# Media keys of the gated layer, for two neighbouring examples at a time

## The reference

```
qn = layernorm(x, ln_q_g, ln_q_b)
q = qn @ Wq * 64 ** -0.5                 # 256 -> 16 heads x 64 = 1024
k, v = split(media @ Wkv)                # 128 -> 1024 each, for 64 media tokens
sim = where(media_mask, q @ k^T, min)    # per head: 256 x 64
out = softmax(sim) @ v
x = x + tanh(attn_gate) * (out @ Wo)
h = gelu(layernorm(x) @ W1) @ W2
x = x + tanh(ff_gate) * h
```

## Time and profile before

| | |
|---|---|
| median of 3 runs | 1388.88 us (1388.78 to 1389.87) |
| profiled execution | 1388.42 us |
| its span | 1386.5 us |
| TensorE busy in the span | 1314.9 us, 95% |
| VectorE, ScalarE, GpSimd busy | 764.6, 473.6, 451.3 us |
| mean granted TensorE clock | 0.98 |

### The profile page before, as it was taken

The page is one execution under the profiler, slowest core; times in us unless marked ns, Lnnn a source line. Parts: engine busy times, 40 slices in busy tenths (PEclk is TensorE's granted clock), DMA queues, the critical chain, the costliest instruction groups (busy, mean ns, idle before and its releaser), DMA issues.

```text
span 1386.5 us, 26030 instructions
## 1 busy us (share of the span) xinstructions
PE 1314.9 (95%) x10995; PEld 1055.5 (76%) x10995; DVE 764.6 (55%) x1361; ACT 473.6 (34%) x785; POOL 451.3 (33%) x558
## 2 busy tenths in 40 slices
PE   7977899999999999999999999989899999999988
PEld 5755677787886777888888888876678787787766
DVE  4455575666666656353344434445667566666553
ACT  3323333423324223244345443433332333313321
POOL 1143444444344332211111111324334344334332
PEclk9978999999999999999999999999999999999999
DMA  9010000000001001200000000011000000000000
GB/s 324 7 61 1 2 2 2 1 2 1 2 6 42 2 20 39 86 17 1 1 0 1 0 1 0 1 41 42 2 2 2 1 17 1 2 16 2 1 17 17
DMA packets 19903, 27.31 MB, mean 20 GB/s; under 512 B 3433, under 2 KB 15553, under 8 KB 19521
## 3 DMA queue, kind: packets, MB, share of 16 engines
q1 hardware_dynamic: 19008, 24.20, 5.2%
q10 hardware_dynamic: 768, 1.26, 0.3%
HBM read 23.35 MB, written 2.10 MB: 18 GB/s over the span
## 4 chain that ended last, share of the span: by engine, by line
PE 84%; DVE 6%; ACT 4%; POOL 3%; issue 2%; DMA 0%; SPq 0%; ACTq 0%; DVEq 0%; POOLq 0%
PE bank L1418 6%; PE bank L1708 6%; PE bank L1673 5%; PE bank L1678 5%; PE bank L1562 5%; PE bank L1914 4%; PE bank L1878 4%; PE bank L1921 4%; PE row_banks L1512 4%; PE row_banks L1822 3%; PE row_banks L1545 3%; PE bank L1480 3%; PE bank L1697 3%; PE bank L1411 3%; PE row_banks L1517 2%; ACT room L2032 2%
## 5 line engine op out<-in xcount | busy, mean ns | idle before, releaser
L1269 POOL TENSOR_SCALAR_AFFINE_SELECT room<-room 128x1024 f32<-128x1024 f32 x64 | 70.7, 1108 | 186.4 <-ACT room L2032 186.4
L2274 DVE TENSOR_REDUCE room<-row_banks 128x4 f32<-128x512 f32 (+1 forms) x128 | 116.4, 952 | 23.4 <-PE row_banks L1517 23.0
L2032 ACT ACTIVATE room<-row_banks 128x1536 f32<-128x1536 f32 x64 | 92.9, 1451 | 89.6 <-PE row_banks L1545 89.6
L1708 PE MATMUL bank<-room,down_w 128*128 128x256 f32 x384 | 94.4, 386 | 0.5 <-DVE room L2374 0.5
L2288 DVE RECIPROCAL room<-bank 128x256 f32<-128x256 f32 x32 | 56.1, 1754 | 59.3 <-PE bank L1562 59.3
L2064 ACT ACTIVATE room<-bank 128x256 f32<-128x256 f32 x96 | 36.4, 383 | 147.7 <-PE bank L1678 136.7
L1231 POOL TENSOR_TENSOR room<-room 128x256 f32<-128x256 f32 x32 | 24.5, 766 | 171.8 <-ACT room L2044 171.8
L1708 PEld LDWEIGHTS bank<-room,down_w 128*128 128x128 f32 x384 | 69.6, 190 | 13.6 <-issue 4.9
L1342 POOL TENSOR_TENSOR room<-room 128x512 f32<-128x512 f32 x32 | 33.7, 1070 | 133.1 <-DVE room L2474 132.9
L1545 PE MATMUL row_banks<-room 32*128 32x256 f32 (+1 forms) x1024 | 62.1, 357 | 9.7 <-ACT room L2032 4.6
L1545 PEld LDWEIGHTS row_banks<-room 32*128 32x128 f32 x1024 | 48.9, 191 | 27.6 <-issue 15.6
(11 more groups left out here) (242 smaller groups left out, 3037.8 us busy)
## 6 DMA issues: line engine op xcount, KB each, us to landing
out_x<-wq SPq DMA_DIRECT2D x8, 256.0 KB, 2.3
qkv<-in_L_xattn_v_qkv SPq DMA_DIRECT2D x2, 768.0 KB, 6.4
qkv<-in_L_xattn_l_qkv SPq DMA_DIRECT2D x2, 768.0 KB, 9.2
gate_w<-in_L_xattn_v_gate SPq DMA_DIRECT2D x2, 640.0 KB, 8.4
gate_w<-in_L_xattn_l_gate SPq DMA_DIRECT2D x2, 640.0 KB, 7.6
up_w<-in_L_xattn_v_up SPq DMA_DIRECT2D x2, 640.0 KB, 6.2
up_w<-in_L_xattn_l_up SPq DMA_DIRECT2D x2, 640.0 KB, 6.5
down_w<-in_L_xattn_v_down SPq DMA_DIRECT2D x2, 640.0 KB, 6.4
```

The lines of the kernel that those rows point to most:

```text
L1269: pool.affine_select(out=diagonal, in_=diagonal, compare_op=ALU.is_ge, fill=0.0, base=0, pattern=[[0, 8], [1, P]], channel_multiplier=-1)\
L1708: return pe.matmul(ff_bank[0][:, t * S:(t + 1) * S], down_w[:, f, t * P:(t + 1) * P], hid[:, i, :], start=(i == t == 0), stop=(i == UPS - ...
L2032: act.activation(probs[w % 2], row_banks[:, :, 0:3 * P], ACT.Exp).then_inc(*ATT_ACT.does(e, f"exp{w}"))
L2274: last = dve.tensor_reduce(dst, row_banks[:, :, P * i:P + S * i], X, ALU.max, negate=True)
```

## The change

The keys of examples e and e+1 (e even) are made together. The moving operand is now the 128 media tokens of both, so eight products of 128 columns replace two times eight of 64. As their result has 1024 columns, it is made in two sets of four products that both go to att_bank: the second set waits until VectorE has taken out the first. Each set is taken out in two instructions as before, now with the two examples as one more dimension. k_diag has 2 x 1024 columns, one half per example; v_diag gets a place of its own, which makes the room 1024 columns larger and adds a memset. Waits are changed to match: a_center and n0_sum wait for a_keys_out only after an even example, otherwise for a_scaled; the scores wait for their own half of the keys; the eviction waits for the scores of the example before that read the same half. In the plan the stages a_keys and a_keys_out now have a list of starts of their own, and stand where they stood for the even examples, the second set 0.1 later on TensorE and 0.3 later on VectorE. In the table of stage names, a_keys now counts `k#` and a_keys_out `k#0 k#1`.

```diff
@@ -787,7 +787,6 @@
     put(-824.5585, "a_centered")
     put(-809.0481, "a_mean")
     put(-808.6594, "a_scaled")
-    put(-804.7289, "a_keys_out")
     put(-803.1344, "a_vals_out", 0)
     put(-790.9899, "a_shift", 0)
     put(-790.6773, "a_vals_out", 1)
@@ -819,7 +818,6 @@
     put(1053.9518, "a_center")
     put(1079.5231, "a_sum")
     put(1088.8030, "a_spread")
-    put(1088.9990, "a_keys")
     put(1089.6066, "a_q", 0)
     put(1090.1252, "a_q", 1)
     put(1090.1254, "a_vals", 0)
@@ -838,6 +836,20 @@
     put(1114.2236, "a_turn", 3)
     put(1122.3099, "a_values", 2)
     put(1122.3100, "a_values", 3)
+    return at
+
+
+def keys_stages():
+
+    at = []
+
+    def put(time, stage, *which):
+        at.append((time, stage, *which))
+
+    put(-804.7289, "a_keys_out", 0)
+    put(-804.4289, "a_keys_out", 1)
+    put(1088.9990, "a_keys", 0)
+    put(1089.0990, "a_keys", 1)
     return at
 
 
@@ -940,6 +952,7 @@
 LATE_STARTS = [[3754.298, 3883.620, 4009.349, 4213.053],
                [4720.064, 4857.234, 4982.216, 5129.719]]
 GATED_STARTS = [4135.764, 4249.007, 4285.180, 4322.416, 4357.961, 4394.327, 4430.914, 4466.419]
+KEYS_STARTS = [4135.764, 4285.180, 4357.961, 4430.914]
 GATED_FF_STARTS = [4379.262, 4415.403, 4452.679, 4488.240, 4524.635, 4561.193, 4596.717, 4630.575]
 FINAL_STARTS = [4340.081, 4340.799, 4473.868, 4474.460, 4603.277, 4604.468, 4766.775, 5969.870]
 
@@ -968,6 +981,7 @@
                      for time, stage, *which in late_stages(layer))
     each(FINAL_STARTS, final_stages(), B)
     each(GATED_STARTS, gated_stages())
+    order.extend((KEYS_STARTS[e // 2] + time, stage, e, *which) for e in range(0, B, 2) for time, stage, *which in keys_stages())
     each(GATED_FF_STARTS, gated_ff_stages())
     return [(stage, e, *which) for _time, stage, e, *which in sorted(order)]
 
@@ -1034,7 +1048,7 @@
         media_u8 = sb("media_u8", [P, B * M], U8)
 
 
-        ROOM = 23828
+        ROOM = 24852
         room = sb("room", [P, ROOM])
 
         def two(ap):
@@ -1077,9 +1091,9 @@
         f_mem = ff_room[:, 2304:3328].rearrange("p (a n) -> p a n", a=4)
         turns = take(6 * KT * S)
         q_sb, k_sb, q_cos, q_sin, k_cos, k_sin = (two(turns[:, KT * S * i:KT * S * (i + 1)]) for i in range(6))
-        k_diag = turns[:, 0:1024].rearrange("p (j i m) -> p j i m", j=GT, i=2)
-        v_diag = turns[:, 1024:2048].rearrange("p (j n) -> p j n", j=GT)
-        a_zero = turns[:, 0:2048]
+        k_diag = turns[:, 0:2048].rearrange("p (b j i m) -> p b j i m", b=2, j=GT, i=2)
+        v_diag = take(GT * P).rearrange("p (j n) -> p j n", j=GT)
+        a_zero, v_zero = turns[:, 0:2048], v_diag
         n0_yl, n0_yv, ff_yl, ff_yv, ctx_v, ctx_l = (take(KT, S) for _ in range(6))
         ff_late = take(KT, 2, M)
         a_yl, a_y, b_yl, b_y = n0_yl, n0_yv, ff_yl, ff_yv
@@ -1326,6 +1340,7 @@
                 def a_zero_pads(e):
                     pool.wait_ge(*QKV_ACT.did(B - 1, "qm1"))
                     pool.wait_ge(*QKV_ACT.did(B - 1, "ka1"))
+                    pool.memset(v_zero, 0.0)
                     pool.memset(a_zero, 0.0).then_inc(*A_POOL.does(e, "zero"))
 
                 def a_add(e):
@@ -1440,7 +1455,7 @@
                         pe.wait_ge(*F_ACT.did(0, "m3"))
                         pe.wait_ge(*X_ACT.did(B - 1, "x"))
                     elif e == B:
-                        pe.wait_ge(*A_DVE.did(B - 1, "k1"))
+                        pe.wait_ge(*A_DVE.did(B - 1, "scaled"))
                     elif e % B > 2:
                         pe.wait_ge(*ATT_DVE.did(e - 3, "ctx1"))
                     sum_squares(n0_sq, att_bank).then_inc(*N0_PE.does(e, "sumsq"))
@@ -1796,7 +1811,7 @@
                     if e == 0:
                         pe.wait_ge(*ATT_DVE.did(B - 1, "ctx1"))
                     else:
-                        pe.wait_ge(*A_DVE.did(e - 1, "k1"))
+                        pe.wait_ge(*(A_DVE.did(e - 1, "k11") if e % 2 else A_DVE.did(e - 1, "scaled")))
                     center(e, att_bank).then_inc(*A_PE.does(e, "mu"))
 
                 def a_sum(e):
@@ -1823,14 +1838,18 @@
                                              start=(k == 0), stop=(k == KT - 1))
                     last.then_inc(*A_PE.does(e, f"q{u}"))
 
-                def a_keys(e):
-                    pe.wait_ge(*A_DVE.did(e, "scaled"))
-                    if e == 0:
-                        pe.wait_ge(ca_in, 16 * CA_DMAS)
-                    for j in range(GT):
-                        last = pe.matmul(att_bank[:, j * M:(j + 1) * M], wkv[:, j * P:(j + 1) * P],
-                                         ctx_t[:, e * M:(e + 1) * M], start=True, stop=True)
-                    last.then_inc(*A_PE.does(e, "k"))
+                def a_keys(e, h):
+                    if h == 0:
+                        pe.wait_ge(*A_DVE.did(e, "scaled"))
+                        if e == 0:
+                            pe.wait_ge(ca_in, 16 * CA_DMAS)
+                    else:
+                        pe.wait_ge(*A_DVE.did(e, "k01"))
+                    for j in range(4):
+                        at = (4 * h + j) * P
+                        last = pe.matmul(att_bank[:, j * P:(j + 1) * P], wkv[:, at:at + P],
+                                         ctx_t[:, e * M:(e + 2) * M], start=True, stop=True)
+                    last.then_inc(*A_PE.does(e, f"k{h}"))
 
                 def a_vals(e, c):
                     pe.wait_ge(*A_ACT.did(e, f"q{c}"))
@@ -1845,12 +1864,12 @@
                     half, t = u // 2, u % 2
                     out = row_banks[:, (2 + u) % 4, :]
                     pe.wait_ge(*A_ACT.did(e, f"q{max(2 * half + 1, 2 + u if u < 2 else 0)}"))
-                    pe.wait_ge(*A_DVE.did(e, "k1"))
+                    pe.wait_ge(*A_DVE.did(e // 2 * 2, f"k{half}1"))
                     if u >= 2:
                         pe.wait_ge(*A_DVE.did(e, f"v{u - 2}1"))
                     for j in range(4):
                         last = pe.matmul(out[:, j * P:(j + 1) * P], a_queries[:, 4 * half + j, t * P:(t + 1) * P],
-                                         k_diag[:, 4 * half + j], start=True, stop=True)
+                                         k_diag[:, e % 2, 4 * half + j], start=True, stop=True)
                     last.then_inc(*A_PE.does(e, f"cs{u}"))
 
                 def a_turn(e, u):
@@ -2434,17 +2453,19 @@
                     dve.wait_ge(*A_PE.did(e, "spread"))
                     dve.tensor_tensor(a_yl, a_yl, both(att_bank[:, 0:S]), ALU.mult).then_inc(*A_DVE.does(e, "scaled"))
 
-                def a_keys_out(e):
-                    dve.wait_ge(*A_PE.did(e, "k"))
+                def a_keys_out(e, h):
+                    dve.wait_ge(*A_PE.did(e, f"k{h}"))
                     if e == 0:
                         dve.wait_ge(*A_POOL.did(0, "zero"))
                     else:
-                        dve.wait_ge(*A_PE.did(e - 1, "cs3"))
+                        dve.wait_ge(*A_PE.did(e - 1, f"cs{2 * h + 1}"))
                     for i in range(2):
                         r = slice(i * M, (i + 1) * M)
-                        dve.tensor_tensor(k_diag[r, :, i, :], att_bank[r, :].rearrange("p (j m) -> p j m", j=GT),
-                                          media[r, e * M:(e + 1) * M].unsqueeze(1).to_broadcast([M, GT, M]), ALU.mult)\
-                           .then_inc(*A_DVE.does(e, f"k{i}"))
+                        seen_keys = media[r, e * M:(e + 2) * M].rearrange("p (b m) -> p b m", b=2)
+                        dve.tensor_tensor(k_diag[r, :, 4 * h:4 * h + 4, i, :],
+                                          att_bank[r, :].rearrange("p (j b m) -> p b j m", j=4, b=2),
+                                          seen_keys.unsqueeze(2).to_broadcast([M, 2, 4, M]), ALU.mult)\
+                           .then_inc(*A_DVE.does(e, f"k{h}{i}"))
 
                 def a_vals_out(e, c):
                     dve.wait_ge(*A_PE.did(e, f"v{c}"))
```

More of the change, by code:

```diff
@@ L149 @@
     "a_scaled": ("a", "dve", "scaled"), "a_affine": ("a", "act", "y0 y1"),
-    "a_q": ("a", "pe", "q#"), "a_q_out": ("a", "act", "q#"), "a_keys": ("a", "pe", "k"), "a_keys_out": ("a", "dve", "k0 k1"),
+    "a_q": ("a", "pe", "q#"), "a_q_out": ("a", "act", "q#"), "a_keys": ("a", "pe", "k#"), "a_keys_out": ("a", "dve", "k#0 k#1"),
     "a_vals": ("a", "pe", "v#"), "a_vals_out": ("a", "dve", "v#0 v#1"),
```

## The result

The changed kernel takes 1384.68 us in the median, the kernel before 1388.88, so that the medians differ by 4.2 us. The ratio of the runs side by side is 0.9966 (95% interval 0.9954 to 0.9979), which is 4.7 us less, between 2.9 and 6.4. The executions lie between 1382.84 and 1385.15 us but for one disturbed one of 1695.83, which the ratio leaves out. The profiled execution took 1382.84 us with a span of 1380.9.

What follows compares the result with a forecast made beforehand. TensorE, busy for 95% of the span, was taken to bound the kernel. The terms -6.92 + 0.15 + 1.67 + 0.13 + 0.99 + 0.06 gave -3.92 us, so 1385.0 us by the median, range 1382.2 to 1388.0.

Steps and rivals of the forecast that it cites:

- Width costs nothing up to 128 columns: TensorE's key products: matmuls of 64 and 128 columns cost the same, 0.108 to 0.111 us each.
- Rival 4: Key products: instructions cost by their columns, 0.216 us for 128, so the change is slower, 1391.7 us; chance 3%.
- Odd examples, 1.73 each: Examples 1, 3, 5, 7 on TensorE lose their 16 key matmuls, 1.73 us each, -6.92 us in all.
- Example 0, +1.67: Between example 0's key sets TensorE waits for VectorE's two evictions and restarts, 1.67 us more.
- Rival 1: Example 0's wait is swallowed by idle time between 530 and 590: -5.6 us, 1383.3 us; chance 10%.
- Example 6, +0.99: a_center of example 7 waits for the pair's last eviction with only one projection between, +0.99 us.
- Examples 2 and 4: Longer key sets +0.05 us each, uncovered eviction +0.13 in example 2, b_joined behind the second eviction +0.03 each.
- rival 3: VectorE's evictions of the keys take longer, 0.848 us each: +1.6 us, 1386.6 us; chance 6%.
- At nothing: GpSimd's larger memset (+0.9 us, idle time behind it), shifted weight loads and scores read from another place cost nothing.
- The clock: Granted clock falls to 0.50 after mostly idle TensorE stretches, losing 2.8 us; the change can make or remove one.
- Rival 5: Two clock falls more, the only new idle place of size at 528: +1.7 us, 1390.6 us; chance 4%.
- rival 2: One clock fall more, 1387.8 us (chance 10%), or one less, 1382.2 us (chance 5%).

Runs made afterwards that it cites:

- e1: Changed kernel with each 128-column key product split into two of 64 columns, order and waits kept: 1391.87 us, ratio 1.0019 against the kernel before.
- e2: Changed kernel with the cross-attention values product of example 7 put between the two key sets of example 0: 1382.45 us, ratio 0.9948 against the kernel before.
- e3: Changed kernel with a_q part 0 of example 6 put before a_center of example 7: 1383.30 us, ratio 0.9955 against the kernel before.
- e6: Kernel before with only the new place of v_diag, the larger room and the memset of 1024 more columns: 1389.49 us, ratio 0.9999.
- e2 to e6: Five runs: e2, e3, both their moves together (1381.70 us), second key set right behind the first in examples 2, 4 and 6 (1388.31 us), and e6.
- e10: The kernel of e1 run once more, unchanged, for its profile: 1393.29 us.

## Why the prediction was right, point by point

The forecast was 1385.0 us, the measured median is 1384.68. The sum for the gated stretch was -3.92 us, the profile has -4.5 us (-4.44 between the marks). The mechanism came out as forecast, but that the total hits to 0.3 us is partly luck. Profile against profile the forecast was 1384.5 and the measured time 1382.84, 5.6 us less than before and not 3.9: 0.6 more in the gated stretch, 1.0 behind it and 0.1 ahead of it. And the single executions differ by what lies ahead of the gated layer: in the four profiles of the changed kernel the first key product starts at 527.0, 531.7, 527.4 and 527.8, while the gated stretch is 367.2 us and the rest 486.7 in each.

- **Width costs nothing up to 128 columns.** Right: 0.89 us for eight, and e1 shows the reverse, narrow products in the new order lose the saving. Rival 4 falls. The Trainium skill, "TensorE: Matmul & The Clock Gate", section "LDWEIGHTS (loading the stationary operand)", has a load take, in ns, its columns divided by 1.2, an estimate of 107 ns here; the trace agrees, with eight loads and their matmuls fewer for 1.73 - 0.89 = 0.84 us, 105 ns each. As a load and a matmul always go together in these runs, it stays open which of the two sets this pace. The cycles that the prediction cites from the section "Back-to-back issue gap" of the same page of the Trainium skill stand there for a product by itself, not for a stream with a load for each, so rival 4 had less behind it than the prediction says.
- **Odd examples, 1.73 each.** They gave 1.78, 1.80 and 1.79, and examples 0 and 1 together fit that too. The term was 0.06 too small each, 0.24 in all. The chain's piece of 1.73 us isn't all that a narrow set costs: what follows it takes 0.05 us more. In example 3 before, behind the keys of the earlier trace rows, the projections are

```profile
674.40 3.51 PE bank L1878 x16
```

where sixteen at 0.216 are 3.46. Without the keys, after the change, the chain has the 28 projections in one piece, and behind a wide set (example 4) twelve take 2.59 us:

```profile
669.91 6.04 PE bank L1897 x28
...
714.86 2.59 PE bank L1897 x12
```

Before it was 2.59 + 1.73 + 3.51 = 7.83 us for the same projections with the keys, 1.79 more. And in e1, at the same place of example 4, twelve take 2.65 behind a narrow set:

```profile
720.54 1.73 PE bank L1851 x16
722.27 2.65 PE bank L1898 x12
```

So 16 narrow matmuls cost 1.78 us and not 1.73, which is also what two wide sets cost.

- **Example 0, +1.67.** 1.69 at the values, a stand of 1.50 us in it, and e2 gets 1.7 back by covering it. Rival 1, that the idle time up to 590 swallows it, is refuted by the same run.
- **Example 6, +0.99.** 0.98 between the marks, a stand of 0.73 us and the restart; e3 gives 0.9 back. (The sum had 0.05 more there for the two sets.)
- **Examples 2 and 4.** I had 0.21 and 0.08 with the longer sets and the two small waits; the marks have 0.04 and 0.01. The sets aren't longer, as just said. In example 2 the weight load waits 0.17 us, but the load runs ahead of its matmul, and the set takes only 0.04 us longer. The restart of 0.20 that I added showed only where the matmul itself stood, in examples 0 and 6. This and the odd examples are why the marks have 0.5 us more than the sum.
- **VectorE.** 0.688 us for an eviction against the 0.69 taken; rival 3 (0.848) didn't occur. b_joined came behind the second eviction as foreseen.
- **At nothing.** The memset of 1024 columns and the new places: e6 shows no difference.
- **A slip.** What still ends between 520 and 590 is layer 1, not layer 0 as the prediction says. No number hangs on it.
- **The clock.** Here the prediction was wrong by its own sign, a fall that comes or goes. The page's slices look the same as before, but one fall more came. Rival 5 named the stand of example 0 as its only place of size. There it didn't come in four profiles of the changed kernel, but it came with narrow products. The new one lies behind the gated layer, where two others became shorter, so that one fall more went with less time at half speed and not with the 2.8 us more of rival 2. The kernel after (windows of 2 us, as the earlier trace rows):

```profile
898.00:900.00 2.00, 0.61 (x4) 0.52 (x4) 0.22 (x2) 2.00 (x4) 1.01 (x2) 1.00 0.00 0
900.00:902.00 2.00, 1.53 (x14) 1.20 (x18) 0.69 (x1) 0.69 (x2) 1.07 (x2) 0.55 0.00 0
902.00:904.00 2.00, 2.00 (x15) 1.14 (x12) 0.24 (x1) 1.98 (x3) 0.00 (x0) 0.60 0.00 0
904.00:906.00 2.00, 2.00 (x20) 1.51 (x22) 2.00 (x4) 0.59 (x2) 0.00 (x0) 1.00 0.03 8
...
1344.00:1346.00 2.00, 2.00 (x6) 1.65 (x5) 0.63 (x1) 0.63 (x1) 0.63 (x1) 0.50 0.00 0
```

The first fall is over by 904, after some 3.4 us, where the kernel before took about 7; the second, at 962, has 3.4 us too, where it was 6.8 at 964 before; the third keeps its 6.8, and a short one at 1344 is new. From the last projection on, the span has 487.7 us before and 486.7 in all four profiles after, but 487.2 to 487.9 in e2 to e6. That is the 1.0 us of the profiled difference that no step of the prediction explains. It goes with the falls: of the twelve profiles, the seven with about 17.0 us at half speed behind the gated layer (the idle end of the program not counted) take 486.7 to 487.2 us there, the five with about 20.5 take 487.3 to 487.9. But no run sets the falls, so it stays argued.

## What to carry to other kernels

Where weights change with every product and the moving operand is narrow, read the price of an instruction by width from the chain, not from its duration. If two widths cost the same, join neighbours until the wider one is full; the win is the number of instructions that go. The joined result fills a bank twice as fast, so look at once for what TensorE does between filling it and filling it again: an eviction of 1.4 us needs 1.7 us of other work there, and two stages moved in the order were worth 2.7 us in the gated stretch on top of 4.5.

## What the runs showed of the hardware that was not expected

After a stand of TensorE of 1.5 us, with 0.50 us busy in a window of 2 us, the granted clock fell from 1.00 to 0.50 in both profiles of one kernel (e1, e10) and stayed at 1.00 in all four of another. What differs ahead of it is the work in the key set, 16 narrow matmuls against 8 wide ones. In the last layer, falls lasted either about 3.4 us or about 6.8, and which it was changed with the kernel.

Sixteen matmuls of 64 columns took 1.73 us in the chain and held up what followed by 0.05 us; eight of 128 columns took 0.89 us and held up nothing. A weight load that waited 0.17 us cost 0.04 us, while a stand of the matmul cost its length and about 0.2 us more.
